# First attention layer: key rows for steps four and six issued before the queries are split, and seven of eight projection units ahead of the first fills

## What is computed

```python
a = _layer_norm(audio_kv, ln_gamma, ln_beta)
Q = (hidden_states @ Wq.T).reshape(B, Tt, HEADS, HEAD_DIM).transpose(0, 2, 1, 3)
K = (a @ Wk.T).reshape(B, Ta, HEADS, HEAD_DIM).transpose(0, 2, 1, 3)
V = (a @ Wv.T).reshape(B, Ta, HEADS, HEAD_DIM).transpose(0, 2, 1, 3)
scores = jnp.einsum('bhtd,bhsd->bhts', Q, K) * scale
attn = jax.nn.softmax(scores, axis=-1)
out = jnp.einsum('bhts,bhsd->bhtd', attn, V).transpose(0, 2, 1, 3).reshape(B, Tt, D) @ Wo.T
return hidden_states + jnp.tanh(gate) * out
```

## Time and profile before

| what | us |
|---|---|
| median of three runs | 1323.19 (1320.06 to 1329.7) |
| profiled execution | 1328.43 |
| its span, first to last instruction | 1326.6 |
| first layer's last TensorE work ends | about 198 |

### The profile page before, as it was taken

How to read it: one execution, slowest core, us unless ns; L and a number is a source line. 1 busy time by engine, 2 the same in 40 slices (tenths; PEclk the granted TensorE clock), 3 DMA queues, 4 the chain that set the end, 5 groups by cost and what they waited for, 6 DMA issues and landing times.

```text
span 1326.6 us, 17919 instructions
## 1 busy us (share of the span) xinstructions
PE 1231.8 (93%) x6064; PEld 863.9 (65%) x6064; DVE 794.0 (60%) x2354; ACT 537.3 (40%) x1233; POOL 216.7 (16%) x429
## 2 busy tenths in 40 slices
PE   7788889898989788999999799999999999999999
PEld 4366555464645343444443588888888888888877
DVE  4443327685858346787785566666666666666620
ACT  3143343343535333555455344334333344343332
POOL 3122005242424211102011100000000000000000
PEclk9798789898999879999999999999999999999999
DMA  7434623101011545533524823030303030500000
GB/s 230 140 111 126 198 90 127 72 32 64 34 63 42 152 146 150 181 126 119 171 75 142 303 86 127 1 127 1 128 1 128 1 128 0 191 1 0 1 8 24
DMA packets 100650, 127.58 MB, mean 96 GB/s; under 512 B 6736, under 2 KB 78576, under 8 KB 98320
## 3 DMA queue, kind: packets, MB, share of 16 engines
q1 hardware_dynamic: 99936, 126.14, 29.1%
q10 hardware_dynamic: 624, 0.30, 0.1%
HBM read 79.33 MB, written 46.79 MB: 95 GB/s over the span
## 4 chain that ended last, share of the span: by engine, by line
PE 78%; DMA 8%; DVE 5%; ACT 3%; POOL 2%; issue 2%; SPq 1%; ACTq 0%; POOLq 0%; DVEq 0%
PE J L2450 8%; PE TT L2458 8%; PE J L2470 8%; PE OO L1079 4%; PE TT L2434 4%; PE S L2424 4%; PE OO L2424 4%; PE OO L1076 3%; PE J L324 2%; PE J L1079 2%; PE S L636 2%; PE J L1345 2%; PE OO L2691 2%; DMA km<-query_parts 2%; PE S L324 1%
## 5 line engine op out<-in xcount | busy, mean ns | idle before, releaser
L2528 ACT ACTIVATE PT<-TT 128x512 f32<-128x512 f32 x128 | 76.4, 597 | 282.8 <-PE TT L2434 282.8
L2563 POOL COPY On<-probs 128x8 f32<-128x8 f32 x128 | 29.2, 228 | 471.3 <-DVE probs L2598 442.1
L2609 DVE TENSOR_SCALAR QK<-J,cols 128x256 f32<-128x256 f32 x126 | 61.0, 484 | 70.4 <-PE J L2450 70.4
L2598 DVE TENSOR_SCALAR probs<-probs,inv 128x257 f32<-128x257 f32 x256 | 79.1, 352 | 4.5
L1079 PE MATMUL OO<-ctxT,weights_a 128*128 128x512 f32 x136 | 69.9, 638 | 12.2 <-SPq L308 9.4
L2434 PE MATMUL TT<-ident,probs 128*128 128x128 f32 x512 | 76.9, 273 | 2.6 <-DVE probs L2598 2.6
L1076 PE MATMUL OO<-weights_a,ctxT 128*128 128x512 f32 x136 | 67.8, 622 | 10.3 <-SPq L308 6.1
L2434 PEld LDWEIGHTS TT<-ident,probs 128*128 128x128 f32 x512 | 63.9, 141 | 16.3 <-DVE probs L2598 3.4
L2604 DVE COPY km<-TT 128x256 f32<-128x256 f32 x128 | 54.2, 424 | 30.8 <-PE TT L2458 30.5
L2317 DVE TENSOR_TENSOR_SCAN early<-km,early 128x256 f32<-128x256 f32 x64 | 64.3, 1045 | 10.9 <-ACT early L2088 10.1
L2458 PE MATMUL TT<-PT,weights_a 128*128 128x256 f32 x256 | 66.6, 383 | 0.0
(11 more groups left out here) (414 smaller groups left out, 2721.5 us busy)
## 6 DMA issues: line engine op xcount, KB each, us to landing
wide_keys<-weights_a SPq DMA_DIRECT2D x64, 256.0 KB, 2.1
wide_values<-weights_a SPq DMA_DIRECT2D x56, 256.0 KB, 2.0
query_parts<-weights_a SPq DMA_DIRECT2D x48, 192.0 KB, 2.8
weights_a<-wide_keys SPq DMA_DIRECT2D x16, 512.0 KB, 7.2
weights_a<-wide_values SPq DMA_DIRECT2D x16, 512.0 KB, 8.3
early<-wide_keys SPq DMA_DIRECT2D x16, 512.0 KB, 8.0
early<-wide_values SPq DMA_DIRECT2D x16, 512.0 KB, 9.3
weights_a<-key_parts SPq DMA_DIRECT2D x16, 288.0 KB
```

Of the source, the lines that this page charges most:

```text
L2528: act.activation(PT[:, n % 2, :], T0[:, :], ACT.Copy).then_inc(pt3_ready, 1)
L2598: ins = dve.tensor_scalar(P_[n % 2][:, qt, :], P_[n % 2][:, qt, :], inv[:, qt, n % 32:n % 32 + 1], None, ALU.mult)
```

## The change

`spread0` is cut in two. For steps 4 and 6 the key rows' transfers (with their wait for the scores of step m - 4) stand at i = 0 of the odd step, ahead of the writes of the query parts at i = 1; the query rows' transfers stay at i = 2. For all other steps both halves are still issued together. Units 5 and 6 leave the loop and run with units 0 to 4, ahead of the first fill; unit 7 stays at at = -1. ACT's copies move with them.

```diff
         def spread0(sp, m):
 
+            spread_keys0(sp, m)
+            spread_queries0(sp, m)
+
+        def spread_keys0(sp, m):
+
             b, first = m // 2, m % 2 * HEADS_AT
             if m >= 4:
                 sp.wait_ge(st0_done, CHUNKS0 * (m - 3))
...
+        def spread_queries0(sp, m):
+
+            b, first = m // 2, m % 2 * HEADS_AT
+            here = slice(first * S, (first + HEADS_AT) * S)
             sp.wait_ge(query0_kept, 16 * 2 * PARTS * (b + 1))
...
                 if n >= 0 and n % 2 == 1 and b + 2 < B:
+                    if i == 0:
+                        spread_keys0(sp, 2 * b + 4)
                     if i == 1:
                         keep_queries0(sp, b + 2)
                     if i == 2:
-                        spread0(sp, 2 * b + 4)
+                        spread_queries0(sp, 2 * b + 4)
...
-                for u in range(FIRST - 3):
+                for u in range(FIRST - 1):
                     if u == 1:
                         pe.wait_ge(values0_ready, 1)
...
-                    if -3 <= at < 0:
+                    if at == -1:
                         u = FIRST + at
                         pe.wait_ge(ahead_copied, u - 1)
                         project_ahead(pe, (J1, O0)[u % 2], u)
...
-                for u in range(FIRST - 3):
+                for u in range(FIRST - 1):
                     copy_first(act, (J1, O0)[u % 2], u)
...
-                    if -2 <= at < 1:
+                    if at == 0:
                         copy_first(act, (J1, O0)[(FIRST + at - 1) % 2], FIRST + at - 1)
```

## The result

The changed kernel takes 1317.05 us (median of 20 runs, 1310.95 to 1330.08), the kernel before 1324.72 in the same comparison (20 runs, 1319.78 to 1331.43). The ratio is 0.9943, 95% interval 0.9921 to 0.9965: 7.5 us less, 5 to 10 by the interval. 8.0 were forecast. The profiled execution took 1320.08 with a span of 1318.3 us, 8.3 less than the span before.

A forecast was written before the change was run, and what follows sets the result against it. TensorE, busy 93% of the time, was taken to bound the kernel with its work and waits, mostly for transfers. With +2.75 absorbed, -3.7 - 2.7 - 1.6 = -8.0 from the median 1323.2 gave 1315.2 us, range 1304 to 1327.

The forecast's parts named there:

- Units ahead of the first fills: Units 5 and 6 end at about 37.93, before rows land at 38.3: no cost, 0.4 us to spare.
- The wait for step 2's rows: Before step 2's fills: the 5 us freed from the loop lengthen the 2.65 us wait to 7.7 at most, no gain.
- The clock's price: Behind step 2's longer wait, work from 66.30 runs at half clock: +2.75 us, bounds nothing to 3.3.
- Key rows of step 4: Issued at 79.3, ahead of the query writes; step 4's fills at 100.0 instead of 103.67 (-3.7), clock held (-2.7).
- Step 6: Query rows land at 129 to 130, a wait of about 2 us replaces 2.61; half of 3.3 booked, -1.6 us.
- Steps 5 and 7: Maxima's transfer, the 3.04 us wait and the 16.7 us at half clock stay as they are: 0.
- The signs of being wrong: First fills after 38.5, step 2's rows not at 66, query writes far over 3.2 us, others at later waits and stretches.
- Held writes: Rival, chance 0.15: key rows hold the query writes about 4 us or more, nothing is won, 1326 us.
- The vanished slow stretch: Rival, chance 0.17: the wait before 151.61 gets short, 16.7 us at half clock become 8.4; 1307 us.

The follow-up runs named there:

- e_keys_only: The changed kernel with units 5 and 6 back in the loop, so the key rows' move alone: 0.9942 of the kernel before, median 1313.92 us.
- e_after_again: The changed kernel measured once more, with nothing altered: 0.9980 of the kernel before, median 1319.81 us.
- e_after_third: The changed kernel measured another time, on one chip with the key rows' move alone: 0.9931 of the kernel before, median 1313.95 us.
- e_units_only: The kernel before with only units 5 and 6 moved ahead of the first fills: 1.0006 of the kernel before, median 1323.88 us.
- e_keys_again: The key rows' move alone, units in their old places, measured again beside the changed kernel: 0.9928 of the kernel before, median 1312.85 us.

## Why the rows are late: three engines

The theory behind the late rows is that key rows run on three engines. In e_rows12 the same bytes go in three transfers of 24 rows, on the changed kernel:

```diff
             for s in range(2):
-                sp.dma_start(k_rows0[m % 4][0:ROWS0, s, :, :],
-                             key_parts0[b, s].rearrange("c (d h) n -> (c d) (h n)", d=HALF0)[:, here]
-                             .unsqueeze(0).to_broadcast([PARTS, PARTS * HALF0, n_here]))\
-                    .then_inc(rows0_landed[m % 4], 16)
+                for r in range(PARTS):
+                    top = PARTS * HALF0
+                    sp.dma_start(k_rows0[m % 4][r * top:(r + 1) * top, s, :, :],
+                                 key_parts0[b, s].rearrange("c (d h) n -> (c d) (h n)", d=HALF0)[:, here])\
+                        .then_inc(rows0_landed[m % 4], 16)
...
-                        pe.wait_ge(rows0_landed[m % 4], 16 * 4 * (m // 4 + 1))
+                        pe.wait_ge(rows0_landed[m % 4], 16 * (2 * PARTS + 2) * (m // 4 + 1))
```

> The changed kernel, with each broadcast of key rows made by three transfers of 24 rows in place of one with an outer dimension of 3; the same bytes. Theory (a broadcast with outer dimension 3 runs on three engines only, at 76 GB/s, share 0.19, and that is what all row waits are): the stretches at share 0.19 vanish, 576 KB of key rows take 2 to 4 us at 150 to 280 GB/s, the first fills start some us before 38.8, step 2's rows land near 58 instead of 66.9, waits for rows fall under 1 us; SP issues four transfers more per step, 2 us. Gain over the kernel before 15 to 25 us, ratio 0.981 to 0.989. Rival (the reading of the same HBM lines, not the number of engines, sets 76 GB/s): the same landing times, ratio 0.994 or worse by the issue time.

Measured: 0.9845 (0.9805 to 0.9885), 1302.37 us: some 20 us less than before. Stretches in which it reads key rows of step 4 (issued at 74.74), and, below, from who waited for whom between 36 and 170 us (total us, times, longest), TensorE's waits for POOL and for transfers:

```profile
75.00:77.00 2.00, 2.00 (x22) 1.60 (x23) 1.71 (x9) 2.00 (x4) 0.00 (x0) 1.00 0.49 141
77.00:79.00 2.00, 2.00 (x27) 1.29 (x20) 1.66 (x10) 1.22 (x3) 0.93 (x2) 1.00 0.61 154
79.00:81.00 2.00, 2.00 (x20) 1.67 (x17) 1.50 (x8) 0.88 (x2) 1.86 (x3) 1.00 0.01 4
...
PE OO L689 <- POOL weights_a L941: 3.1, 2, 2.6
PE TT L664 <- DMA km<-weights_a: 2.5, 1, 2.5
...
PE TT L664 <- DMA early<-weights_a: 1.2, 1, 1.2
```

Key rows now take 4 us at 141 to 154 GB/s, and the DMA engines are idle by 79, where 576 KB at the 76 GB/s of before need some 8 us. Every wait for key or query rows is gone from the list; both transfers in it are the maxima's. The rival, that reading the same lines three times sets the rate, has fallen: they are still read three times. The Trainium skill ("DMA: Bandwidth & Descriptors", section "Why a DMA increments its semaphore by 16 and not by 1") says that a transfer issued from SP or ACT runs on the largest number of engines, up to 16, that divides the slowest dimension of both sides. By that rule 3 and 72 give three engines, 24 and 24 give twelve; the trace agrees, with share 0.19 before and up to 0.61 here, which is ten of sixteen engines at least.

Does the change still pay on top? e_rows12_before has this edit on the kernel before:

> The kernel before (neither part of the change), with each broadcast of key rows made by three transfers of 24 rows. Theory (key rows on three engines are what the change works around): the wait of 6.93 us is gone without any reordering, since key rows behind the writes take 3 us in place of 8; ratio 0.984 to 0.987, within 0.003 of e_rows12. Rival (order and engines each give their own part): ratio 0.990, the change still worth 7 us on top.

Measured: 0.9871 (0.9838 to 0.9903), 1302.21 us. In its trace TensorE waits for no key or query rows between 36 and 170 us, with SP's queue in its old order. With twelve engines the order of key rows and queries' parts is worth nothing that these runs can tell; the change works around the three engines. The third of this kind puts the units back:

> Key rows by three transfers of 24 rows, key rows of steps 4 and 6 ahead of the queries' parts, units in their old places (five ahead, three in the loop). Theory (with rows that land early, units 5 and 6 ahead of the first fill are no longer covered): first fill near 36 instead of 39.3 us, step 0's maxima 3 us earlier; the units then cost 3 us in the loop instead of 3.4 ahead of it: ratio within 0.002 of e_rows12 (0.9845). Rival (the units' place decides the clock of 50 to 65 us): 0.982.

Measured: 0.9855 (0.9823 to 0.9888), 1300.25 us, the fastest median of all. Its first fill is at 34.26, in e_rows12 at 39.30, without a bracket in either. Of these 5.0 us, 1.9 stand already at the first unit (25.36 and 27.29); the rest is the two units. So with rows that land early, units 5 and 6 do stand on the path ahead of the first fill, as the prediction priced it (3.4). From the first fill to the first scores it is 19.1 us here and 17.7 in e_rows12: in that part of the loop their move gives 1.4 us back. The ratios don't tell the two apart.

## The rows of maxima

What is left is the wait for the maxima's rows, 12 KB that took 7.88 us before. e_maxima8 sends them in three transfers of one row, with the key rows' move alone (the waits on `max0_landed` count three times as many):

```diff
-                    act.dma_start(q_rows0[m % 4][ROWS0:ROWS0 + PARTS, 1, :, :], max_rows0).then_inc(max0_landed, 16)
+                    for r in range(PARTS):
+                        act.dma_start(q_rows0[m % 4][ROWS0 + r:ROWS0 + r + 1, 1, :, :],
+                                      max_rows0[r * HEADS_AT:(r + 1) * HEADS_AT, :]).then_inc(max0_landed, 16)
```

> The key rows' move alone (units in their old places), with each transfer of the maxima's rows cut into three of one row, from eight partitions each. Theory (the maxima's rows, 12 KB, take 5 to 8 us since they wait on the three engines that the key rows fill; over eight engines more of them are still the same loaded ones, and it doesn't matter how small the pieces are): the wait before step 5's scores stays at 2 to 4 us in loaded stretches, ACT issues 1.5 us more per step; ratio within 0.002 of e_keys_only. Rival (three engines with 4 KB each are the reason): maxima land in 2 to 3 us, no wait for them anywhere, the slow stretch behind 145 us gone in all runs, times in one heap near 1308 to 1312, ratio 0.989.

Measured: 0.9953 (0.9923 to 0.9982), 1318.28 us. ACT's queue and what waited for it:

```profile
51.62 2.89 ACTq L847 DMA_DIRECT2D km<-weights_a  x3
...
60.12 0.60 PE L663 MATMUL TT<-km,weights_a 72*128 72x256 bf16 x4 [1.42 <-DMA km<-weights_a]
```

From 51.62 to 60.12 is 8.5 us, no less than the 8.2 of the changed kernel (issued at 52.04, scores at 60.28); 1.3 us of it are the longer issue (2.89 us for three transfers, 1.56 for one). Three pieces don't bring the 2 to 3 us of the rival. Nor do key rows on twelve engines bring them, as the chain of e_rows12 shows for step 5's maxima:

```profile
126.81 7.76 DMA km<-weights_a
```

There the DMA share is 1.03 from 130 to 134 us, so all engines are loaded, and not three by key rows. A trace without such load is that of the kernel before at step 7: its maxima are sent at 177.75, the DMA share is 0.03 and then 0.00, and its first scores start without a wait:

```profile
182.30 0.61 PE L651 MATMUL OO<-early,weights_a 72*128 72x256 bf16 x4
```

So the same 12 KB landed in 4.6 us at most. The load makes the transfer longer; in which way it does, these runs don't show. Both edits together:

> Key rows by three transfers of 24 rows, key rows of steps 4 and 6 ahead of the queries' parts, units in their old places, and the maxima's rows by three transfers. Theory: as e_rows12_units5 (0.9855), the last wait of 2.6 us for step 5's maxima stays. Rival: that wait is gone, and with it up to 8 us of slow clock in some runs: ratio 0.980 to 0.983.

Measured: 0.9864 (0.9835 to 0.9892), 1303.55 us, no better than e_rows12_units5. It still waits 1.46 and 1.64 us for maxima.

## Why the prediction was right, step by step

The number was right, and so was the main mechanism: key rows ahead of the query parts remove the wait before step 4's fills and the half clock behind it. Several terms were off, in both directions, and that they add up to the measured 7.5 us is in part luck.

**Units ahead of the first fills, right in this trace.** They ended at 34.75 + 1.88 = 36.63, the rows landed at 38.8: covered, by 2.2 us rather than 0.4, as the units began sooner in this execution. In the two other profiles of the changed kernel the units began 2.5 to 2.7 us later; in e_after_again 0.56 us of wait were left before the first fill, in e_after_third none.

**The wait for step 2's rows, wrong in its place.** I put the freed 5 us into one wait of 7.7 us before step 2's fills. 3.29 us stand before the first scores and 0.47 before the fills. The step that failed: I went from the units straight to step 2's rows and didn't ask what the first scores, which stand between, wait for. Before, they waited for ACT's copy of unit 7 (the row at 60.38). Behind it was the transfer of step 0's maxima, issued at 52.04 and landed at 60.28 here; before it was issued at 51.62, and with the same 8.2 us it would have landed at 59.9, hidden by half a microsecond (an estimate from these rows). The fills of step 2 were at 66.89, before at 66.30.

**The clock's price, right in this trace and no further.** +2.75 was the term; from the issue of step 2's key rows to the first write of query parts it was 31.24 us before and is 34.38, +3.1. The shares were otherwise: the clock fell towards the end of the 3.29 us wait, stayed at 0.50 from 59.6 to 73, and the part before 66.3 was hidden by the remaining wait. But the same distance is 33.6 to 37.5 us in the three other profiles that have the units ahead and leave the gap (e_units_only, e_after_again, e_after_third), and 31.3 to 34.4 in those that have them in their old places: e_keys_again has 34.43, with the clock at half behind step 2's fills and no unit moved. So the price lies inside what the same place varies by from one execution to the next, and the times couldn't confirm it either.

**Key rows of step 4, right in time, the term too large.** Issued at 79.33 (forecast 79.3), writes at 86.42 (85.6), query rows issued at 93.84 (94.3). The first of these agrees by luck: I had the key parts' landing and the shift give it, while step 0's last scores, 3.6 us later than before, ended only at 79.30. The fills started at 101.86, not 100.0, as TensorE came late: another 6.6 us at half clock (90.9 to 97.5) followed the POOL wait of 2.67 us, 3.4 us of which the kernel before had too. So -1.8 for -3.7. That the clock would hold behind it, -2.7, was right: 1.00 from 97.6 to 144.9. Together it is -4.1 for -6.4 (the transposes behind these fills start at 105.40, before at 109.51).

**Step 6, right, the term too small.** Fills at 131.99 with a wait of 2.14 us, forecast 129 to 130 with 2. The clock held; I had booked half of its 3.3 us. The fills are 7.5 us sooner than before, of which 3.4 arise here for the 1.6 that were booked. With step 4's 4.1 that is 7.5 where 8.0 was forecast: two errors that cancel.

**Steps 5 and 7, the term too small.** I booked nothing. Step 5's wait for maxima is 3.64 us (before 3.04), its transfer 8.90 us, the stretch at half clock 20.1 us instead of 16.7, and 1.8 of the 7.5 us are lost again. The first layer ends 5.7 us sooner; the rest of the 8.3 in this pair of profiles, 2.6 us, comes from later stretches, where the prediction had nothing. Without them the sum would have been 2.3 us too large.

**The signs of being wrong.** Of those that I named, the first fills came after 38.5 (38.80, but for late rows and not for the units), SP issued step 6's writes in far more than 3.2 us (6.57), and the stretch at half clock after 150 had another length. The number came out right in spite of them.

**Rivals.** Held writes: for step 4 they are not held. From their first issue to the issue of the query rows, which wait for their landing, it is 7.4 us (86.42 to 93.84), before 7.2 (82.86 to 90.08). There the key rows are issued 7.1 us ahead of the writes. For step 6 they are only 3.8 us ahead, and it is 10.3 us (116.27 to 126.61), before 5.5 (120.38 to 125.92): held by 4.8 us, as I had estimated (4.5), and more than the 4 from which I let the rival decide. That was taken from step 4's place; at step 6 it ended in the wait of 2.14 us, in place of the 2.61 for maxima. The vanished slow stretch didn't come in the changed kernel's profile (20.1 us); e_keys_only's shows what it would be, with 13.4 us at half clock and none after 144.

## What to carry to other kernels

Look at the DMA share of a stretch in which one kind of transfer is alone: 0.19 is three of sixteen engines, and there the shape of the transfer is to be changed before its place in the queue; here that gave 20 us where the reordering gave 7. When work is moved into a wait, name every release of the instruction that it stood in front of, those too that are hidden by half a microsecond. And before a price of 3 us is read out of one pair of profiles, look at how far the same distance varies between profiles of one kernel.

## What the hardware showed that was not expected

A 12 KB transfer on ACT's own queue took 8 to 9 us with SP's transfers in flight (7.88, 8.90), 7.76 with key rows on twelve engines, and 8.5 in three pieces; with the DMA engines idle it was 4.6 at most. The clock's stretches are long against the waits that stand before them: 3.64 us idle, then 20.1 us at 0.50 with TensorE busy throughout; but behind 2.14 us at 131.99 none at all. The changed kernel's times span 16 us in twelve executions and 19 in twenty, more than the whole effect of this change.
